# Decoder layer on one core: second context's half sums made by transfers, its spectra placed before the last head turn

## The reference, cut to what matters

```python
qf = rfft(x1 @ Wq.T); kf = rfft(ctx @ Wk.T)
corr = irfft(qf * conj(kf)).mean(features of a head)
weights, delays = top_k(corr, 6); w = softmax(weights)
out = sum_i w_i * roll(v, delay_i)      # v = ctx @ Wv.T
x2 = layernorm(x1 + out @ Wo.T + bo)
```

## Time and profile before

| quantity | value |
|---|---|
| median of three runs | 595.45 us |
| the profiled execution's own time | 596.93 us |
| its span | 595.1 us |
| TensorE matmul busy | 522.4 us, 88% |
| VectorE busy | 447.8 us, 75% |
| ScalarE busy | 260.9 us, 44% |
| GpSimd busy | 123.0 us, 21% |
| mean granted TensorE clock | 0.964 of full speed |

### The profile page before, as it was taken

The page is one execution under the profiler, slowest core; times in us unless marked ns, Lnnn a source line. Parts: engine busy times, 40 slices in busy tenths (PEclk is TensorE's granted clock), DMA queues, the critical chain, the costliest instruction groups (busy, mean ns, idle before and its releaser), DMA issues. The chain is left out here.

```text
span 595.1 us, 16615 instructions
## 1 busy us (share of the span) xinstructions
PE 522.4 (88%) x7294; PEld 404.6 (68%) x7294; DVE 447.8 (75%) x870; ACT 260.9 (44%) x478; POOL 123.0 (21%) x110
## 2 busy tenths in 40 slices
PE   8876879888998998989798889699999799998993
PEld 5544766777677776777664345488878678787883
DVE  3995867786787778787385999974985968758874
ACT  3765545442445244434246445433423245364441
POOL 1001640062006201701202012205770001000000
PEclk9998879999999999998899998999999999999998
DMA  7700830161016101613144101142000000001102
GB/s 202 226 24 1 228 93 3 39 178 39 3 50 178 30 4 35 182 31 83 54 161 150 35 1 35 37 176 89 0 1 1 1 2 0 1 1 36 36 1 71
DMA packets 51383, 37.48 MB, mean 63 GB/s; under 512 B 4657, under 2 KB 46642, under 8 KB 51311
## 3 DMA queue, kind: packets, MB, share of 16 engines
q1 hardware_dynamic: 51039, 36.16, 20.6%
q10 hardware_dynamic: 272, 0.26, 0.1%
HBM read 34.31 MB, written 2.10 MB: 61 GB/s over the span
## 5 line engine op out<-in xcount | busy, mean ns | idle before, releaser
L322 DVE SCALAR_TENSOR_TENSOR arena<-bank,conv_w,arena 128x511 f32<-128x511 f32 (+2 forms) x72 | 53.0, 746 | 12.4 <-ACT arena L490 9.0
L1560 POOL COPY arena<-v_win 128x256 f32<-128x256 f32 x32 | 21.4, 698 | 158.8 <-PE bank L812 158.7
L1227 ACT COPY arena<-bank 128x512 f32<-128x512 f32 x40 | 21.7, 589 | 46.7 <-PE bank L938 46.7
L2127 ACT COPY arena<-bank 128x512 f32<-128x512 f32 x38 | 21.6, 585 | 38.2 <-PE bank L1871 28.5
L1871 PE MATMUL bank<-v_win,arena 128*128 128x256 f32 x160 | 37.8, 382 | 0.6 <-ACT arena L2127 0.6
L1182 ACT COPY arena<-bank 128x256 f32<-128x256 f32 x32 | 19.4, 606 | 36.4 <-PE bank L829 36.4
L1871 PEld LDWEIGHTS bank<-v_win,arena 128*128 128x128 f32 x160 | 30.0, 190 | 5.3 <-ACT arena L2127 1.0
L923 PE MATMUL bank<-arena 64*64 64x32 f32 x1280 | 24.7, 224 | 8.5 <-DVE arena L1449 3.4
L725 PE MATMUL bank<-arena 128*128 128x512 f32 x64 | 31.2, 609 | 0.9 <-PEq L728 0.9
L923 PEld LDWEIGHTS bank<-arena 64*64 64x64 f32 x1280 | 22.0, 138 | 11.4 <-DVE arena L1449 6.7
L2261 ACT CAST h_hi<-arena 128x512 fp32r<-128x512 f32 x24 | 14.9, 621 | 30.6 <-DVE arena L2572 30.6
(11 more groups left out here) (306 smaller groups left out, 1406.0 us busy)
## 6 DMA issues: line engine op xcount, KB each, us to landing
arena<-in_toep_w SPq DMA_DIRECT2D x32, 256.0 KB, 3.3
arena<-in_toep_l SPq DMA_DIRECT2D x32, 256.0 KB, 3.8
arena<-in_xT SPq DMA_DIRECT2D x12, 512.0 KB, 4.7
arena<-in_x SPq DMA_DIRECT2D x4, 512.0 KB, 4.1
out<-arena SPq DMA_DIRECT2D x4, 512.0 KB, 2.9
arena<-in_ctx SPq DMA_DIRECT2D x3, 512.0 KB, 4.1
v_win<-in_w_gateT SPq DMA_DIRECT2D x1, 768.0 KB, 5.2
v_win<-in_w_upT SPq DMA_DIRECT2D x1, 768.0 KB, 6.7
```

The source lines that it names most:

```text
L322: return nc.vector.scalar_tensor_tensor(out=acc[:, j:L], in0=src[:, 0:L - j], scalar=conv_w[:, m, CONV_K - 1 - j:CONV_K - j], in1=acc[:, j:L],
L1227: nc.scalar.copy(A2["XT"][:, 2 * th:2 * th + 2, :, :], turn_bank(th)[:].rearrange("p (t e c) -> p t e c", t=2, e=2)).then_inc(s2["xt_out"] ...
L1560: g.tensor_copy(A2["v_piece"][:, n % 2, :, :].rearrange("p c (t two) -> p t two c", two=2), v_win[:, :, :, n * BATCHED:(n + 1) * BATCHED]. ...
L2127: nc.scalar.copy(dst(i), bank[RING_FIRST + n % RING].rearrange("p (t c) -> p t c", c=dst(i).shape[-1]))\
```

## The change

1. The mixing: `weigh(b)` is reordered (plain and short first, then wide, long, their sum, delta, delta plus that sum). The add of the plain product onto the short one, a VectorE instruction, becomes an accumulating transfer from one SBUF tile onto another, issued by GpSimd (`plain_onto_short`). VectorE waits for it ahead of the two last adds.
2. The second context (b = 1): SyncE loads its upper half into the rows of the short branch of sequence 0, which are free then; ScalarE writes a copy with the sign turned beside it (`second_negative`); two accumulating transfers from HBM add the lower half onto both (`second_sums`), which gives sum and difference. Its transform isn't refolded. `ctx_sums(1)` goes; `ctx_sums(2)` and `ctx_sums(3)` stand together where it stood, ahead of `norm_roots(3)`. The three feed-forward weight loads now wait for `project_v(1)`.
3. Order: `project_v(0)` moves ahead of `forward_x(0)`; `forward_ctx(1)`, `project_k(1)`, `project_v(1)` move ahead of `turn_o(3)`; the copies of ScalarE follow.
4. The bias onto `x1` (`with_bias`) becomes four accumulating transfers, one after the other, in place of four GpSimd adds.
5. `inverse(1)` moves ahead of `correlation(1)`, `project_o(1)` ahead of `turn_delays(1)`, `output_out(1)` ahead of `evens_out(1)`, `output_sum(1)` ahead of `best(1)`.

```diff
         def spectrum(b, kind, i):
 
-            return SPECTRA * b + 2 * (KINDS if b else FIRST_KINDS).index(kind) + i
+            return SPECTRA * b + 2 * KINDS[b].index(kind) + i
+        half_of_ctx = lambda b, half: dr["ctx"][b].rearrange("(a t p) d -> a p t d", a=2, p=P)[half]
...
+                sp.wait_ge(s3["p_v"].sem, s3["p_v"].at(0, 2))
+                sp.dma_start(second_ctx[:, 2:4, :], half_of_ctx(1, 1)).then_inc(s4["ctx_in1"].sem, 16)
                 sp.wait_ge(s3["p_wl"].sem, s3["p_wl"].at(B - 1, 2))
-                load_ctx(1)
                 load_ctx(2)
+                load_ctx(3)
                 sp.wait_ge(s3["p_v"].sem, s3["p_v"].at(B, 0))
+                sp.wait_ge(s4["spec_mm"].sem, spectrum(1, "v", 1) + 1)
                 for w, (n, k) in zip(ffn, (("w_gateT", KT), ("w_upT", KT), ("w_downT", MF))):
-                    if n == "w_downT":
-                        sp.wait_ge(s4["spec_mm"].sem, spectrum(0, "v", 1) + 1)
                     sp.dma_start(w.bitcast(I32).rearrange("p (k n) -> p k n", k=k),
                                  dr[n].rearrange("(k p) n -> p k n", p=P)).then_inc(ffn_in.sem, 16)
-                load_ctx(3)
...
                         for par in range(1 if refolded(b, kind) else 0, 2):
+                            rows = second_ctx[:, 2 - 2 * par:4 - 2 * par, :] if (b, kind) == (1, "c") else src[:, par, :, :]
                             for k in range(2):
-                                i = mm(o[:, par * 256:(par + 1) * 256], src[:, par, k, d * P:(d + 1) * P],
+                                i = mm(o[:, par * 256:(par + 1) * 256], rows[:, k, d * P:(d + 1) * P],
                                        dft[:, k, par * 256:(par + 1) * 256], start=(k == 0), stop=(k == 1))
                 def forward_ctx(b):
-                    if b:
-                        pe.wait_ge(s4["ceo"].sem, s4["ceo"].at(b - 1, 4))
+                    if b >= 2:
+                        pe.wait_ge(s4["ceo"].sem, s4["ceo"].at(b - 2, 4))
+                    elif b:
+                        pe.wait_ge(s4["second_sums"].sem, s4["second_sums"].at(0, 32))
...
                         project_k(0)
+                        project_v(0)
                         forward_x(0)
-                project_v(0)
                 forward_x(1)
+                forward_ctx(1)
+                project_k(1)
+                project_v(1)
                 turn_o(B - 1)
                 project(B - 1)
-                forward_ctx(1)
                 project_q(1)
-                project_k(1)
-                project_v(1)
                 forward_x(2)
                 forward_ctx(2)
                 project_q(2)
                 project_q(3)
                 project_k(3)
                 inverse(0)
+                inverse(1)
                 correlation(1)
-                inverse(1)
                 project_o(0)
+                project_o(1)
                 turn_delays(1)
-                project_o(1)
                 forward_delays(1)
                 pe.wait_ge(s4["res4"].sem, s4["res4"].at(0, 2))
                 project_v(3)
...
+                def second_negative():
+
+                    act.wait_ge(s4["ctx_in1"].sem, s4["ctx_in1"].at(0, 16))
+                    a(second_ctx[:, 0:2, :], second_ctx[:, 2:4, :], ACT.Copy, scale=-1.0).then_inc(s4["second_neg"].sem, 1)
                 def output_out(b):
+                    if b == 1:
+                        act.wait_ge(s4["prod"].sem, s4["prod"].at(B - 1, 4))
                         nc.scalar.copy(eb_of(b)[:, m, :], ot_bank(b, m)[:, 0:HALF]).then_inc(s4["eb_out"].sem, 1)
                         norm_out(b - 1)
+                    if b == 1:
+                        second_negative()
                         k_out(0)
+                        v_out(0)
                         x_out(0)
                     if b < B - 1:
                         turned_out(b)
@@ -2221,14 +2234,13 @@
-                v_out(0)
                 x_out(1)
+                ctx_out(1)
+                k_out(1)
+                v_out(1)
                 turned_out(B - 1)
                 norm_out(B - 1)
-                ctx_out(1)
                 q_out(1)
-                k_out(1)
-                v_out(1)
                 x_out(2)
                 ctx_out(2)
                 q_out(2)
                 output_out(0)
+                output_out(1)
                 evens_out(1)
-                output_out(1)
                 exps(1)
                 ffn_weights()
...
                     dve.wait_ge(s3["lg_post"].sem, s3["lg_post"].at(b, 5))
-                    for f, n in enumerate((WIDE, LONG)):
-                        v.tensor_tensor(by_head(A3[u]["pwl"][:, f, :, :]), branch(n, b), part(2 - f), ALU.mult).then_inc(s3["p_wl"].sem, 1)
-                    v.tensor_tensor(by_head(A3[u]["pd"]), branch(DELTA, b), part(3), ALU.mult).then_inc(s3["p_sd"].sem, 1)
                     if b >= 2:
                         dve.wait_ge(s3["o_turned"].sem, s3["o_turned"].at(b - 2, 2))
                     v.tensor_tensor(by_head(A3[u]["pv"]), branch(PLAIN, b), part(4), ALU.mult).then_inc(s3["p_v"].sem, 1)
+                    if b >= 2:
+                        dve.wait_ge(s3["x1_out"].sem, s3["x1_out"].at(b - 2, 4))
+                    v.tensor_tensor(by_head(A3[u]["ps"]), branch(SHORT, b), part(0), ALU.mult).then_inc(s3["p_v"].sem, 1)
+                    v.tensor_tensor(by_head(A3[u]["pwl"][:, 0, :, :]), branch(WIDE, b), part(2), ALU.mult).then_inc(s3["p_wl"].sem, 1)
+                    v.tensor_tensor(by_head(A3[u]["pwl"][:, 1, :, :]), branch(LONG, b), part(1), ALU.mult).then_inc(s3["p_wl"].sem, 1)
                     dve.wait_ge(s3["p_wl"].sem, s3["p_wl"].at(b, 2))
                     v.tensor_tensor(A3[u]["pwl"][:, 0, :, :], A3[u]["pwl"][:, 0, :, :], A3[u]["pwl"][:, 1, :, :], ALU.add)\
                         .then_inc(s3["p_wl"].sem, 1)
-                    if b >= 2:
-                        dve.wait_ge(s3["x1_out"].sem, s3["x1_out"].at(b - 2, 4))
-                    v.tensor_tensor(by_head(A3[u]["ps"]), branch(SHORT, b), part(0), ALU.mult).then_inc(s3["p_sd"].sem, 1)
-                    dve.wait_ge(s3["p_wl"].sem, s3["p_wl"].at(b, 3))
-                    dve.wait_ge(s3["p_sd"].sem, s3["p_sd"].at(b, 1))
+                    v.tensor_tensor(by_head(A3[u]["pd"]), branch(DELTA, b), part(3), ALU.mult).then_inc(s3["p_wl"].sem, 1)
+                    dve.wait_ge(s3["p_wl"].sem, s3["p_wl"].at(b, 4))
                     v.tensor_tensor(A3[u]["pd"], A3[u]["pd"], A3[u]["pwl"][:, 0, :, :], ALU.add).then_inc(s3["o_sum"].sem, 1)
-                    dve.wait_ge(s3["p_v"].sem, s3["p_v"].at(b, 1))
-                    dve.wait_ge(s3["p_sd"].sem, s3["p_sd"].at(b, 2))
-                    v.tensor_tensor(A3[u]["ps"], A3[u]["ps"], A3[u]["pv"], ALU.add).then_inc(s3["p_sd"].sem, 1)
                     dve.wait_ge(s3["o_sum"].sem, s3["o_sum"].at(b, 1))
-                    dve.wait_ge(s3["p_sd"].sem, s3["p_sd"].at(b, 3))
+                    dve.wait_ge(s3["p_vs"].sem, s3["p_vs"].at(b, 16))
...
                 def products(b):
-                    dve.wait_ge(s4["spec_out"].sem, spectrum(b, "k" if b else "q", 1) + 1)
+                    dve.wait_ge(s4["spec_out"].sem, spectrum(b, "k" if b >= 2 else "q", 1) + 1)
                 output_sum(0)
+                output_sum(1)
                 best(1)
-                output_sum(1)
                 delays_turned(1)
                 residual4(0)
...
                 def ctx_sums(b):
                     c, ceo = ctx_of(b), ceo_of(b)
                     pool.wait_ge(s4[f"ctx_in{b % 2}"].sem, s4[f"ctx_in{b % 2}"].at((b - 1) // 2, 16))
-                    if b >= 3:
-                        pool.wait_ge(s4["spec_mm"].sem, spectrum(b - 2, "c", 1) + 1)
                     g.tensor_tensor(ceo[:, 1, :, :], c[:, 0:2, :], c[:, 2:4, :], ALU.subtract).then_inc(s4["ceo"].sem, 1)
-                    pool.wait_ge(s4["ceo"].sem, s4["ceo"].at(b - 1, 1))
+                    pool.wait_ge(s4["ceo"].sem, s4["ceo"].at(b - 2, 1))
                     g.tensor_tensor(c[:, 0:2, :], c[:, 0:2, :], c[:, 2:4, :], ALU.add).then_inc(s4["ceo"].sem, 1)
-                    pool.wait_ge(s4["ceo"].sem, s4["ceo"].at(b - 1, 2))
+                    pool.wait_ge(s4["ceo"].sem, s4["ceo"].at(b - 2, 2))
                     g.tensor_tensor(ceo[:, 0, 0, :], c[:, 0, :], c[:, 1, :], ALU.add).then_inc(s4["ceo"].sem, 1)
                     g.tensor_tensor(ceo[:, 0, 1, :], c[:, 0, :], c[:, 1, :], ALU.subtract).then_inc(s4["ceo"].sem, 1)
                 def with_bias(b):
                     pool.wait_ge(s4["xeo"].sem, s4["xeo"].at(b, 4))
-                    g.tensor_tensor(x1_of(b), x1_of(b), over_tiles(xo_b[:], TT), ALU.add).then_inc(s4["x1b_out"].sem, 1)
+                    if b:
+                        pool.wait_ge(s4["x1b_out"].sem, s4["x1b_out"].at(b - 1, 16))
+                    g.dma_start(x1_of(b), over_tiles(xo_b[:], TT), accum_op=ALU.add).then_inc(s4["x1b_out"].sem, 16)
...
```

(33 more changed lines are left out.)

17 lines of the change are left out of this document (8 added, 9 removed).

## The result

The changed kernel takes 600.55 us in the median, the kernel before 596.31 us in the runs made beside it. The ratio is 1.0061 with a 95% interval of 1.0042 to 1.0080: slower by 3.6 us, give or take 1.1. The profiled execution took 601.47 us, its span is 599.5 us.

The account below looks back on a forecast made before the run. VectorE paces the mixing, TensorE is nearly full from 400 to 440 us, and the loop from the last turn to forward_x(2) decides. -1.0 (A) + 8.8 (B and C) - 2.5 (D) = +5.3 us: forecast 600.8 us, range 595 to 607.

Parts of the forecast that it names:

- A: Mixing: a transfer replaces one VectorE add per sequence; -1.0 us in all, bounds -3.4 to +7.1.
- D: Adjacent inverses, from inverse(0) to the first feed-forward product: no idle ahead of correlation(1); -2.5 us.
- C: From the turn to forward_x(2): VectorE's 16.3 against TensorE's 9.5 us leaves 6.8 us idle, then slow clock; +8.8 us.
- Rival 1: Mixing: the transfer is slow, towards 9.2 us; total +13.4 us, 608.9 us; chance 0.17.
- B: Spectra up to the turn of sequence 3: it starts at 422.6 in place of 409.67, 13.0 us later.
- E: Second context, negated copy, bias transfers, weight loads: 0.8 us more TensorE time, hidden; the transfers end before they are needed.
- Rival 2: Whole kernel: mixing transfer hidden, no clock fall after the idle; +1.2 us, 596.7 us; chance 0.18.
- Rival 3: Ahead of forward_x(2): the gap doesn't open; -5.6 us, 589.9 us; chance 0.10.

Follow-up runs that it names:

- e3: Changed kernel with the mixing's add of plain and short products back on VectorE, no transfer in the mixing; ratio to before 1.0165.
- e12: Changed kernel with plain and short products behind wide and long, leaving two VectorE instructions between the mixing transfer's issue and its wait; ratio to before 1.0242.
- e1: Changed kernel with sums(2) between head_norm(3) and residual(3), right behind the turn, in place of behind products(0); ratio to before 0.9948.
- e8: Kernel before with only the four bias adds turned into accumulating transfers; ratio to before 1.0034.
- e5: Changed kernel with only forward_ctx(1) ahead of turn_o(3); project_k(1) and project_v(1) go behind project_q(1); ratio to before 0.9886.
- e9: From e5: forward_ctx(1) between turn_o(3) and project(3), project_v(0) back in front of forward_x(1); 585.64 us, ratio to before 0.9818.
- e2: Changed kernel with forward_ctx(1), project_q(1), project_k(1) and project_v(1) behind project(3) again; ratio to before 0.9979.
- e6: e5 with sums(2) right behind the turn as well, as in e1; ratio to before 0.9908.
- e10: The kernel of e5 measured once more; ratio to before 0.9878.

## Why the prediction was right, and where its terms were off

The forecast was +5.3 us. The stretches give +2.8, the runs +3.6 (2.5 to 4.8), so the sum was too high by about 2 us: A by 2.4 and D by 0.8, while C was too low by 0.6. The mechanism, a gap in front of forward_x(2) with a slow clock behind it, was as forecast. That the median of 600.55 lies so close to 600.8 is in part luck: the kernel before had a median of 596.31 in the later runs and not 595.45.

**A, -1.0 forecast, -3.4 measured.** The direction and the bound were right, the value taken was not: the transfer was put at 6.5 us and lands in 4.8, issue included. Part 6 of the page has the transfer, and VectorE's timeline no wait ahead of the adds behind it:

```profile
arena<-arena POOLq DMA_DIRECT2D x4, 512.0 KB, 4.8
```

```profile
371.30 1.22 DVE L2370 TENSOR_TENSOR arena<-arena 128x1024 f32<-128x1024 f32 x1
372.56 1.29 DVE L2375 TENSOR_TENSOR arena<-arena 128x512 f32<-128x512 f32 x2
```

Together the steps that added time for the second operand and for the issue were too much: 4.8 us is 0.7 more than the 4.1 of a load of that size. The cover of 5.7 us holds it, with at least 0.5 us to spare. That the gain is then 3.4 us, the bound of the forecast (3 x 1.13), is a coincidence. Up to its last adds a mixing takes 8.32 us in place of 9.28, which is 1.0 us less and not 1.13, three times 2.9. The other 0.5 us is a wait of VectorE for ScalarE's exponentials in the softmax of sequence 2, 0.49 us at 362.67, which the kernel before has and the changed one hasn't (in e3 it is 0.76 us; why it goes is open).

Rival 1 was doubted because nothing else uses the DMA engines then. That isn't so for sequence 0, whose transfer is followed by SyncE's loads after 3.5 us; e12 shows the same transfer beside them.

The Trainium skill's fit (DMA: Bandwidth & Descriptors, "Anatomy of one DMA") gave 3.2 us for an issue from GpSimd; the trace shows 4.8, so the measurement decides, though for A both come out the same, since both lie under the cover. e12 shows where it would have differed: with 2.3 us of cover the fit leaves, as an estimate, 0.9 us of wait, and the trace shows 2.6 and more.

**B, right.** The turn was expected 37.7 us after project_k(0) and stands 37.5 after it. The idle ahead of project_k(1) is 1.29 us, forecast 1.7.

**C, +8.8 forecast, +9.4 measured.** VectorE's 16.3 us from the turn to the end of sums(2) came out as 16.3 (420.68 to 436.97), the gap as 6.73 us against 6.8. The clock cost 2.2 us and not 1.7, and of the 0.5 us that were to be saved at the copies some 0.2 came. e1 shows the gap and the slow clock removed together by one edit on VectorE. e8 bears out that GpSimd's adds are what slows VectorE. The Trainium skill's rule (SBUF — State Buffer, "Who interferes with whom") agrees with that, by an instruction of the same shape at 0.68 and 2.83 us. The forecast named two causes for the quick sums(2), the bias transfers and the earlier ctx_sums; e8 shows that the first alone makes sums(2) quick, but leaves the adds of ctx_sums beside what follows, and TensorE waiting for them. In the changed kernel ctx_sums(2) and (3) are done by 418.0, before the late turn, and so keep GpSimd off VectorE behind it.

**D, -2.5 forecast, -3.3 measured.** From inverse(0) on:

```profile
475.10 7.07 PE L1933 MATMUL bank<-v_win,arena 128*128 128x256 f32 x32
482.10 2.81 PE L1901 MATMUL bank<-v_win,arena 128*32 128x256 f32 x16
484.84 7.17 PE L1949 MATMUL bank<-v_win,arena 128*128 128x256 f32 x32
...
493.43 1.97 PE L1918 MATMUL bank<-arena,v_win 128*128 128x32 f32 x16 [0.38 <-DVE arena L2503]
...
505.11 0.82 PE L1981 MATMUL bank<-x_lo,w_gate 128*128 128x512 f32 x2
```

correlation(1) follows without idle at 2.81 us, as forecast, and the pair of inverses takes 7.0 us, not 7.3. The feed-forward stage starts 30.0 us after inverse(0), forecast 30.8. Of the 0.8 us, 0.5 come from VectorE: inverse(2) needs weighted(2), whose last instruction runs from 501.00 to 501.68, and begins 26.7 us after inverse(0), forecast 27.2; inverse(2) itself is 0.25 us shorter. Beside weighted(2) TensorE has a slow clock that the forecast didn't have:

```profile
495.23 1.31 PE L1874 MATMUL bank<-v_win,arena 128*128 128x256 f32 x4
...
500.89 1.04 PE L1964 MATMUL bank<-c_ident,short 128*128 128x128 f32 x8
```

project_v(3), from the first to the second of these rows, takes 5.66 us in place of 3.9, at a granted clock of 0.70. It costs nothing: in e1 the same piece runs at full clock, TensorE then waits for ScalarE's copy and for weighted(2) (0.74 and 0.54 us), and inverse(2) begins 26.7 us after inverse(0) all the same.

**E.** The negated copy takes 0.62 us at 363.86 and holds up nobody. The bias transfers go out at 433.07, 439.10, 445.03 and 450.95, 5.4 us each, done by 456.4 where 471 had been the bound. The weight loads go out at 420.93. The last stretch is unchanged (94.39 against 94.34).

**The rivals.** Rival 1 (a slow transfer) didn't come about. Rival 2 had one half right, the hidden transfer, and one wrong, the clock. Rival 3 rested on the gap not opening; it did, and e1, e5 and e9 show that it decides: without it the same parts are 0.5, 1.2 and 1.8% faster than before. What the forecast didn't say is that the gap was cheap to avoid: it took the late turn, 11 us behind its input, as a consequence and didn't ask which of VectorE's queued pieces could run in the idle ahead of the residual (15.03 us measured).

Still open: why the slow clock lasts longer behind the same idle in e8 than before, and whether e8's loss is more than that. The transfers that make the second context's sums were not tried by themselves: every kernel that has them has part of the reordering too, so what they cost or give isn't shown; e9 shows that a kernel with them can keep TensorE busy from project_k(0) to correlation(0).

## What to carry to other kernels

When a piece that starts a long loop between two engines is moved back, add up both sides of the loop behind it; the difference, here 16.3 - 9.5 = 6.8 us, came back as idle time plus a slow clock, though the moved pieces ran as planned. Put one piece of work over each wait instead of all of them in front of one: the same parts gave 600.6 us with forward_ctx(1), project_k(1) and project_v(1) all ahead of the turn, and 585.6 with project_v(0) shortly ahead of it and forward_ctx(1) right behind it. And when whole spans scatter by several us in stages that nobody touched, compare the lengths between fixed instructions.

## What the runs showed of the hardware that I had not expected

- An adding transfer within SBUF, 512 KB, issued by GpSimd, lands 4.6 to 5.1 us after the start of its issue (0.92 to 1.07 us of GpSimd); beside loads of 512 and 256 KB issued in the same moment, 7.8 us. The one with a repeated 1 KB row as its source (the bias) takes 5.4 to 5.5 us in the changed kernel. In e2, e5, e6, e9 and e10 SyncE issues three loads of 768 KB within 5 us of one of the four, and that one lands after 9.8 to 10.9 us; in e5 it is issued at 429.03 and the loads at 428.10, 428.51 and 430.04.
- What an idle time costs in clock doesn't follow from its length. correlation(1) took 5.34 us in e8 and 4.27 in the kernel before, both behind 3.13 us of idle. project_v(3) took 5.66 us in the changed kernel and 4.1 in e1 (485.92 to 490.05); the last idle ahead of it was 0.38 us in both, in front of forward_delays. project_k(0) took 5.67 us in e9 behind 2.55 us of idle (384.24 to 389.91) and 3.9 in e12 behind 2.23 (where earlier products of L1846 at 387.21 had run slowly, 1.06 us for 0.61).
- The stages ahead of the first softmax differ by up to 5.8 us between executions of kernels that are the same in them, the lengths behind it by 0.2 us.
